# New order tables for two attention layers, and an expert's first weights fetched before the plan is complete

## What is computed

```python
x = x + attention0(layernorm(x))      # x: 16 sequences x 512 x 256, f32; 16 heads of 16; window of 128, rotary
x = x + experts(layernorm(x))         # 8 experts, top 2 of each token, silu(a)*b, 512 wide
x = x + attention1(layernorm(x))      # causal, xpos rotary, biases
x = x + layernorm(x) @ (scale * ternary(W))
```

## Time and profile before

| | |
|---|---|
| time, median of 3 runs | 2713.08 us (2712.34 to 2715.16) |
| the profiled execution | 2714.14 us, of it the span of the trace 2712.2 us |
| busy | PE 2406.1 us (89%), DVE 1752.9 (65%), ACT 1354.6 (50%), POOL 900.5 (33%) |
| mean granted PE clock | 0.947 of full speed |
| stage a0 | 0 to about 945 us; a period (one sequence) is about 53.4 us |
| stage e | about 950 to 1583 us, PE 98% busy |
| stage a1 | about 1589 to 2712 us; a period is about 62.7 us |

### The profile page before, as it was taken

The page is one execution under the profiler, slowest core; times in us unless marked ns, Lnnn a source line. Parts: engine busy times, 40 slices in busy tenths (PEclk is TensorE's granted clock), DMA queues, the critical chain, the costliest instruction groups (busy, mean ns, idle before and its releaser), DMA issues. The chain is left out here.

```text
span 2712.2 us, 50761 instructions
## 1 busy us (share of the span) xinstructions
PE 2406.1 (89%) x17551; PEld 1655.8 (61%) x17722; DVE 1752.9 (65%) x5775; ACT 1354.6 (50%) x2419; POOL 900.5 (33%) x847
## 2 busy tenths in 40 slices
PE   4899999999999489999999946898999999999996
PEld 2465566556665379889888833455555555555553
DVE  4777877887786454444454426777777777777761
ACT  2465666656665233333333312465566665665564
POOL 1446545654652300000000033444444444444300
PEclk8899999999999789999999966899999999999998
DMA  4676776677643577877787634455444444454420
GB/s 149 196 221 209 226 213 213 215 226 224 199 151 101 200 259 274 287 276 280 262 285 247 236 123 139 142 151 144 126 133 126 125 126 129 139 147 127 132 56 16
DMA packets 259616, 490.19 MB, mean 181 GB/s; under 512 B 25608, under 2 KB 191112, under 8 KB 249416
## 3 DMA queue, kind: packets, MB, share of 16 engines
q1 hardware_dynamic: 241944, 435.23, 51.2%
q0 software_dynamic: 17456, 52.19, 5.7%
HBM read 299.65 MB, written 186.52 MB: 179 GB/s over the span
## 5 line engine op out<-in xcount | busy, mean ns | idle before, releaser
L900 ACT ACTIVATE a_pr<-a_bank 128x512 f32<-128x512 f32 (+1 forms) x1152 | 637.4, 574 | 387.0 <-PE a_bank L1323 254.6
L1184 DVE CUSTOM_DVE_ANT_0 a_junk<-a_bank,a_smask 128x256 bf16<-128x256 f32 (+3 forms) x1536 | 651.5, 463 | 131.8 <-PE a_bank L1420 126.7
L1464 PE MATMUL a_bank<-a_pr,a_va 128*32 128x256 f32 (+3 forms) x4096 | 349.2, 417 | 22.0 <-ACT a_pr L900 14.4
L1781 PE MATMUL e_bank<-e_xh,e_under 128*128 128x512 f32 (+1 forms) x1248 | 361.4, 375 | 1.4 <-DVE e_xl L1757 1.4
L1420 PE MATMUL a_bank<-a_kst,a_qst 96*128 96x128 bf16 (+3 forms) x1024 | 266.0, 314 | 30.7 <-DVE a_nmax L1184 12.8
L1323 PE MATMUL a_bank<-a_mask,a_identb 128*128 128x128 bf16 (+2 forms) x981 | 279.8, 285 | 0.0
L1446 PE MATMUL a_bank<-a_qst,a_kst 98*128 98x512 bf16 (+3 forms) x1024 | 253.8, 305 | 12.2 <-ACT a_pr L900 10.7
L1781 PEld LDWEIGHTS e_bank<-e_xh,e_under 128*128 128x128 f32 x1248 | 222.2, 189 | 40.7 <-DVE e_xl L1757 1.8
L1781 PE MATMUL e_bank<-e_xl,e_under 128*128 128x512 f32 (+1 forms) x624 | 233.1, 374 | 0.0
L1668 POOL DMA_DIRECT2D results_dram<-e_yt x39 | 29.3, 753 | 612.6 <-DVE e_yt L1736 595.1
L1691 ACT ACTIVATE e_sa<-e_bank,e_b 128x512 f32<-128x512 f32 (+1 forms) x156 | 101.5, 651 | 247.3 <-PE e_bank L1781 225.6
(11 more groups left out here) (214 smaller groups left out, 5004.9 us busy)
## 6 DMA issues: line engine op xcount, KB each, us to landing
e_under<-ws_dram SPq DMA_DIRECT2D x39, 2048.0 KB, 9.0
a_parts_dram<-a_parts SPq DMA_DIRECT2D x224, 256.0 KB, 3.1
e_under<-ws_dram SPq DMA_DIRECT2D x39, 1024.0 KB, 6.0
e_under<-a_parts_dram SPq DMA_DIRECT2D x96, 384.0 KB, 6.7
a_kst<-a_parts_dram SPq DMA_DIRECT2D x96, 384.0 KB, 9.8
a_parts_dram<-a_parts SPq DMA_DIRECT2D x32, 768.0 KB, 5.9
ws_dram<-a_ws SPq DMA_DIRECT2D x24, 1024.0 KB
a_qst<-a_parts_dram SPq DMA_DIRECT2D x64, 384.0 KB, 8.9
```

The lines of the kernel that those rows point to most:

```text
L900: nc.scalar.activation(pr[b][:, h:h + per, :], TB_[at % 2][:, 0:per * w].rearrange("p (h w) -> p h w", h=per), ACT.Exp, scale=scale).then_ ...
L1184: last = nc.vector.tensor_tensor_reduce(junk[:, at % 2, j * w:(j + 1) * w], SB_[at % 2][:, j * w:(j + 1) * w], smask[:, T - w:T], scale=-1 ...
L1464: last = nc.tensor.matmul(PVB[32 * j:32 * (j + 1), q0:q0 + w], va[i % 2][:, b, (g * HG + j) * VW:(g * HG + j) * VW + 32], pr[b][:, j, :], ...
L1781: last = nc.tensor.matmul(out[:, 0:s.columns], first(s.slot, low)[:, kc, col:col + P], x[s.slot][:, kc, 0:s.columns], start=(p == 0), stop ...
```

## The change

1. `T` and `PV` get entries of their own: `main0` to `main3` now place only `T`, and 16 new entries `PV00` to `PV33` place `PV` by group and block. All numbers of PLACES, EDGES and LAGS are new, for both attention stages.
2. The first tile's expert is found by itself, right behind the third instruction of the plan, and SP waits for this number alone.

```diff
 PLACES = {
     "a0": {
-        "main0": (-0.0444, 0.13257), "sums0": (0.1739, 0.0078), "flip0": (0.2083, 0.0002), "scale0": (0.6025, 0.00057),
+        "main0": (-0.1079, 0.12745), "sums0": (0.2888, 0.00032), "flip0": (0.4686, 0.00128), "scale0": (0.5255, 0.0009),
...
+        "tables": (0.0974, 0.00062), "pads": (-0.1295, 0.00166), "PV00": (-0.0212, 0.00683), "PV01": (-0.0125, 0.0072),
...
-                        put(i, "main" + str(g), step, k)
+                        put(i, "main" + str(g) if step[0] == "T" else "PV" + str(g) + str(step[3]), step, k)
...
-                sp.wait_ge(planned, 1)
-                first_weights(sp, sp.value_load(tile_tab[0:1, 0, 0:1], min_val=0, max_val=NE - 1))
+                sp.wait_ge(first_known, 1)
+                first_weights(sp, sp.value_load(first_expert[0:1, 0:1], min_val=0, max_val=NE - 1))
...
+                then(nc.vector.tensor_scalar(rest, numbers_, -1.0, float(NE), ALU.mult, ALU.add))
                 for i in range(2):
                     then(nc.vector.scalar_tensor_tensor(many[:, i * NE:(i + 1) * NE, :], along(taken[:, :], NJ),
                                                         (i - 1) * TILE / 2, across(full, NE), ALU.add, ALU.is_gt))
                 then(nc.vector.tensor_reduce(units, many, AX.X, ALU.add))
+                then(nc.vector.scalar_tensor_tensor(rest, units[:, 0:NE], 0.5, rest, ALU.is_gt, ALU.mult))
+                then(nc.vector.tensor_reduce(last_, rest, AX.X, ALU.max))
+                then(nc.vector.tensor_scalar(last_, last_, -1.0, float(NE), ALU.mult, ALU.add))
+                nc.vector.tensor_copy(first_expert[:, :], last_[0:1, 0:1]).then_inc(first_known, 1)
...
-                copied_to_steps(who_, 0).then_inc(planned, 1)
+                copied_to_steps(who_, 0)
```

More of the change, by code:

```diff
@@ L123 @@
     "a0": {
[8 rows of a table removed]
-        "minus1": (0.1, 0.01408), "back": (0.0514, 0.03071), "out": (0.1886, 0.00042), "add": (0.1657, 0.00232),
-        "stats2": (0.243, 0.00068), "aggr2": (0.234, 0.05041), "norm2": (0.3091, 0.00433), "y": (0.3155, 0.01993),
-        "turn2": (0.4488, 0.00273), "score": (0.6608, 0.00246), "exp2": (0.6953, 0.01414), "place": (0.7844, 0.00273),
-        "gates": (0.7214, 0.00557), "spots": (0.8174, 0.01468), "scatter": (-0.1442, 0.04986), "fetch0": (0.0593, 0.02034),
-        "high0": (0.2859, 0.00373), "rest0": (0.1832, 0.01828), "keep0": (0.2137, 0.00014), "fetch1": (0.3854, 0.00661),
@@ L141 @@
+        "vcopy": (0.0004, 0.0034), "minus0": (0.6265, 0.0282), "load": (0.5567, 0.00517), "aggr": (0.5592, 0.00361),
+        "stats": (0.7065, 0.00016), "norm": (0.0887, 0.00591), "turn": (0.2145, 0.00014), "stack": (0.8814, 0.00414),
[5 rows of a table added]
     },
     "a1": {
[8 rows of a table removed]
-        "minus1": (0.1158, 0.06305), "back": (0.08, 0.00566), "out": (0.13, 0.0072), "add": (0.1262, 0.00613),
-        "stats2": (0.1994, 0.00694), "aggr2": (0.2785, 0.00232), "norm2": (0.2747, 0.01033), "y": (0.3071, 0.02303),
-        "turn2": (0.3648, 0.00979), "last": (0.4473, 0.00021), "final": (0.4285, 0.01229), "v": (0.024, 0.04954),
@@ L216 @@
-            "gates": (0.5719, 0.00557), "norm2": (0.2405, 0.00361), "pads": (-0.3637, 0.01151), "scale3": (0.1594, 0.00104),
-            "scatter": (0.6182, 0.01096), "score": (0.6254, 0.00901), "spots": (1.1048, 0.00947), "stats2": (0.2537, 0.006),
-            "turn2": (0.5346, 0.02141), "y": (0.1423, 0.03986),
+            "add": (0.2141, 0.02057), "aggr2": (0.6156, 0.00885), "back": (-0.0191, 0.03101), "exp2": (0.7948, 0.09757),
+            "flip3": (-0.1415, 0.00037), "gates": (0.7365, 0.0002), "norm2": (0.2823, 0.05193), "out": (0.2816, 0.00141),
```

84 lines of the change are left out of this document (42 added, 42 removed), and 199 rows, old and new, of tables (EDGES, PLACES).

## The result

The changed kernel took 2628.69 us (2621.6 to 2631.64, 4 runs), the kernel before 2713.35 us: a ratio of 0.968 (95% interval 0.966 to 0.970), 85 us faster. The forecast was 44 us faster, 2670 us, with a range that ended at 2640: the direction was right, the size was not, and, as the stages show, neither was its division. On two other chips the same change gave nothing; that is told with the experiments.

A forecast was written before the change was run, and what follows sets the result against it. It took PE's idle time as what could move: waits for DVE's rotation in a0, for gathers' round trip in a1. Terms -14 (a0), -24 (a1), -3 (handover), -3 (a1's start) made -44, 2670 us; range 2640 to 2708.

The forecast's parts named there:

- a1, -24 us forecast: Second attention stage: DVE asks earlier for gathered rows, 27 us less waiting against 3 us of new waits; bounds 0 and -37.
- The round trip stays 8.77 us: In a1: a gather's time from request to landing unchanged, DVE's distance between halves 7.7 us instead of 5.6.
- a0, -14 us forecast: First attention stage: -13.6 for a rotation wait, -7.5 for short waits, +7 for new waits; bounds 0 and -36.
- `turn2`'s 13.6 us: In a0: PE's wait for DVE's rotation ahead of the normalised tile's turn, taken as wholly gone.
- the third I took: In a0: of 22.6 us of PE's short waits for maxima and exponentials, 7.5 us were to go.
- new waits: In a0: the new order makes waits of its own, 0.5 us in each of 14 periods, 7 us.
- The handover, -3 us forecast: From a0 to the experts: earlier weights shorten the first rows' load by 3.2 us, plan 1 us longer; bounds +1, -5.
- Rival D: From a0 to the experts: early weights delay the last scatters, the handover gives nothing, 2673 us; chance 0.03.
- The start of a1, -3 us forecast: At a1's start: half of DVE's 6.46 us wait for the load of x is saved; bounds 0 and -5.
- A: In a1: the gather stays the bound, request or landing delayed, a1 gives about -3, 2690 us; chance 0.22.
- B: In a0: the late weight chunk fetch holds ACT's exponentials; 2699 us if mild, 2729 us if slower, chance 0.13 for slower.
- C: Both attention stages: a0's waits only swapped, a1 gains little, 2709 to 2719 us, within 0.2% of before; chance 0.07.

The follow-up runs named there:

- mix_early: The changed kernel with a1's second-half mixes placed 0.08 of a period earlier on DVE: 2769.2 us, 1.003 of the kernel before on that chip.
- before_again: The kernel before, unchanged, run once more on chip 0 for a second trace: 2708.8 us.
- five_buffers: The kernel before with five buffers for a1's gathered rows instead of four, second-half gathers 0.04 of a period earlier: 2708.9 us, 0.983 of before.
- half_late: The changed kernel with a0's first-half minus later, by 0.04 of a period on DVE, 0.02 on PE: 2605.4 us, 0.961 of before on chip 0.
- plan_only: The kernel before with only the early search for the first expert, all order tables old: 2756.2 us, 1.000 of before on chip 5.

## Why the prediction was wrong

**a1, -24 us forecast, -82 to -90 measured.** The step that failed is "The round trip stays 8.77 us, so the wait falls by 2.1 us where it was 3.17", and with it "so each of the 13 waits loses 2.1 us". The mechanism was named rightly (DVE's distance between the two halves against the gather's round trip), but both sides moved further: the distance is 9.3 us instead of 7.7, and the round trip is 6.9 us or less (`mix_early`), since the gathers now stand ahead of the stacks in time; that the stacks are the reason is argued from their order and the full DMA engines, not shown. So the waits vanished. At 36.6 us I even had them as the bound, but this bound was no bound. In the windows PE's idle time fell from 4.4 to 1.6 us a period (63.25 x 61/880, 57.5 x 21.4/780). The clock, a term that I put at nothing without a reason although 0.97 stood in the earlier trace rows, gave some 2 us more (57.8 us at half clock became 3.4). That makes 4.8 of the 5.75 us by which the period fell, against 1.9 in the forecast; the last microsecond is open. With `before_again` in place of the first trace it is 2.3 and 1.4 us of 5.1. `five_buffers` shows the same two parts with one buffer changed: 2.0 us of wait and 1.0 to 1.4 of clock for 3.2 to 3.8 us of period. The chain of waits had an upper end for all of it: one landing of 8.7 us in each period, 122 us in all. And 33 of the 90 us lie outside the ten periods, at the stage's start and end, where I had set 3.

**a0, -14 us forecast, +5 measured (experts' first rows).** Right: `turn2`'s 13.6 us went, and more of the short waits went than the third I took. Wrong: "with the longest wait of the PV kind, 0.5 us, once in each of 14 periods, 7 us" for new waits. It was one of 2.1 us, 27.5 us in 13 times, and behind it the clock, which I had left out of the sum although it was in the row (0.99). I had the rule that explains it in hand and applied it to `mix` alone, which it hardly touched (0.476 us in the median, 1.10 at most); `minus`, with the spread of the cast in the earlier trace rows, was the instruction to follow. The cast itself has one input, so its spread was no case of the sentence that I set beside it. `half_late` gives 25 us back, about as much as its shorter waits and its higher clock explain.

**The handover, -3 us forecast, -1.4 in the traces, nothing that `plan_only` could tell.** The landing was right to 0.6 us (3.8 instead of 4.4). On the other side the barrier opens 2.4 us later behind `e_row`, where the sum had +1.0 - 0.7. Rival D, to which I gave 0.03, said that the early weights delay the last scatters. Their issue is not later, but from the last scatter's end to SP's DMA it is 7.0 us instead of 4.5, and on another chip 6.9 in `plan_only` and 4.5 in `five_buffers`. That the scatters land late behind 3 MB of weights would explain it and is argued, not shown; the plan's end is 0.8 us later, too.

**The start of a1, -3 us forecast.** DVE's first rotation starts 34.2 us behind the first load instead of 37.3 (1628.79 and 1594.58, 1627.64 and 1590.34): 3.1 us, as forecast. From the first load to the sixth 19 us went, some 17 of which are three periods' worth at 5.8; what the earlier start gave in the end cannot be told apart.

**The rivals.** A did not come: in the even part no gather waits at all. B did not either: ACT waited for a weight chunk once in the stage, 3.7 us, and never again. C was not what happened even in a0: the idle time did fall, and the clock took more than that back. That the whole could come to nothing on another kind of chip (0.999, 1.001) was nowhere in the forecast; it is C's time, by a0 losing there what a1 gains.

## What to carry to other kernels

Where a transfer lies in a loop of steps, take its price from the chain of waits (its share of the stage) as the upper end, and PE's listed wait as the lower one; here they were 8.7 and 2.8 us a period and the truth was 5.75. Do not hold a transfer's time fixed when the order of the other queues changes: look what stands ahead of it. When an order changes, look for each small DVE instruction with two inputs in SBUF that newly stands beside a long POOL instruction, and what stands behind it on DVE; price PE's wait behind it with the clock that it loses, not by its length alone. And measure an order on more than one chip before keeping it: the sum of two stages was -3% on one and 0 on two others.
